# Batch 0's score maxima in two halves of heads on 64 partitions, and eight of its scores in the opening of each layer

## The chip, the cores and the metric

One core of a Trainium2 chip runs the kernel. The metric is the device time of one launch in microseconds, the median of three runs. A profile of one execution gives the rows quoted below; their times count from the start of its span. TensorE is written PE there, with its weight loads as PEld; VectorE is DVE, ScalarE is ACT, GpSimd is POOL, and SyncE (SP) only issues transfers.

## The reference, cut to what matters

Two layers of gated cross attention, each followed by a gated feed-forward part, on x of 4 batches x 512 queries x 128 channels, with a context of 154 keys, 16 heads of 8 channels. Layer 1 is causal.

```python
x = x + tanh(g_xattn[0]) * L0_xattn(layernorm(x), ctx, ctx)   # softmax(q k^T / sqrt(8)) v, 16 heads
x = x + tanh(g_ffn[0])   * L0_ffn(layernorm(x))               # quantised gate/up/down, needs maxima over all of x
x = x + tanh(g_xattn[1]) * L1_xattn(layernorm(x), ctx, ctx)   # the same with a causal mask
x = x + tanh(g_ffn[1])   * L1_ffn(layernorm(x))               # an LSTM-like scan over the batches
```

Every softmax is taken with its row maximum subtracted, so for each query and head the maximum over the keys is needed before the exponential.

## The kernel before

**Layout.** Heads are numbered h = 4g + j. Query tile Q4 and key tile Kd have 128 partitions = four strips of 32, one for each j; in a strip, 8 channels x 4 rows, which hold the query's high part twice, its low part, and (row 3 of each four) minus the maximum. Kd is a diagonal: for head (g, j) only strip j is filled and the other 96 partitions are zero, so a matmul over all 128 partitions gives one head's scores. There are three Q4 and three Kd tiles, used in rotation by the batches.

**Maxima.** For each batch, `scores_for_top` (L952) multiplies on TensorE one query tile of 128 queries with the keys of up to three heads (a unit: 462 columns of one PSUM bank; a unit that crosses a group g is two matmuls, for example 154 + 308). `UNITS` lists them: 22 for a batch of layer 0. In layer 1 there are 20, and those of the first 256 queries add a causal mask by a second matmul (L956). Three banks (`MRING`) rotate. `take_top` (L1323) reduces each bank on VectorE to `nm`. When the last is done, `split_top` (L1334, L1336) splits `nm` in a high and a low part `nms`; `turn_top` (L966) transposes them on TensorE; `copy_top` (L762) copies them on ScalarE to `nmT`; and SyncE's `tops` (L445) sends them into row 3 of each four in Q4, signalling `m_in`.

**Scores.** Then `scores` (L984, and L990 for the 26 keys left, "tail") makes 20 banks of 512 columns for the batch, on two rotating PSUM banks, `exps` (L771) takes each through the exponential on ScalarE into a ring of eight, and `weigh` (L1016) multiplies four at a time with the values, a "round", in shape 128x32, four column groups side by side.

**Order.** It is written out by hand. For each layer, a turn i runs from -1 to 4 with 20 slots each; turn i holds the scores of batch i and the maxima of batch i + 1, and the last three slots a first part of the maxima of batch i + 2 (8 units for batch 1). Turn -1 is the **opening**: only maxima of batch 0, with projections, values and, after each unit, a filler matmul (`fill`, L1082, 128 partitions, result unused). `PE_PLAN`, `ACT_PLAN` and `DVE_PLAN` place the rest by slot and batch. Engines execute in this order and wait on semaphores:

```python
if t == 0:
    pe.wait_ge(m_in[n % 3], 2 * 16 * (n // 3 + 1))          # scores: the batch's maxima have landed
...
if k >= MRING:
    pe.wait_ge(top_red, k - MRING + 1)                      # units: bank reduced three units before
```

**GpSimd** clears tiles, adds biases to the values (L580, L584), and for layer 1 zeroes masked exponentials (L619).

## Time and profile before

| | us |
|---|---|
| runs | 343.91, 344.22, 344.16; median 344.16 |
| profiled execution | 343.68, its span 341.7 |
| PE busy | 279.8 (82%) |
| DVE busy | 252.4 (74%) |
| ACT busy | 192.5 (56%) |
| POOL busy | 136.4 (40%) |
| DVE maxima, L1323, 168 reductions | 96.0, 626 ns each |
| ACT exponentials, L771, 148 | 82.3, 583 ns each |
| PE maxima, L952, 240 matmuls | 69.7 |
| PE scores, L984, 119 matmuls | 54.4 |

The difference between the profiled execution's time and its span, 2.0 us, lies outside the first and last instruction. Matmuls overlap, so the duration of one (some 0.4 us) is more than the distance from its start to the next one's start; where the text speaks of what a matmul takes, it is that distance. A load row stands at the moment at which the engine starts it, which is normally when the matmul ahead starts, so the load hides behind that matmul.

### The profile page before, as it was taken

To read this page: it belongs to the slowest core of one execution; us is meant where nothing else is said; L and a number is where in the kernel's file an instruction comes from. 1 tells how busy PE (TensorE), PEld (TensorE's weight loads), DVE (VectorE), ACT (ScalarE), POOL (GpSimd) and SP (SyncE) were. 2 spreads that over 40 slices of the span, in tenths; PEclk is the share of its full clock that TensorE was granted. 3 is DMA by queue.
4 is the path that set the end of the run, shared out by engine and by line. 5 is a ranking of instruction groups with operands and counts; after the bars stand their busy time and mean duration, and the time that the engine had idled before them with its cause. 6 is when DMAs were issued, how large, how long until landed. Compare 5 with 4: busy or idle time off the path is not lost. (4 is left out here: it accounts for less than half of the span.)

```text
span 341.7 us, 4467 instructions
## 1 busy us (share of the span) xinstructions
PE 279.8 (82%) x1424; PEld 161.2 (47%) x1424; DVE 252.4 (74%) x538; ACT 192.5 (56%) x303; POOL 136.4 (40%) x274
## 2 busy tenths in 40 slices
PE   0889899899989779985007888899998998999994
PEld 0558544545434355331006776574554653433552
DVE  5699876878997288799989968985696692442833
ACT  1673366566466656679589632356556546664232
POOL 6669893750040411860002059911486107140100
PEclk9999999999999999995556999999999999999998
DMA  7930100110000000000000002220011000000004
GB/s 209 326 150 3 69 32 10 41 60 9 1 10 1 0 2 0 1 0 0 1 0 0 2 14 78 94 101 1 10 59 48 2 0 11 0 1 2 0 1 123
DMA packets 9687, 12.55 MB, mean 37 GB/s; under 512 B 896, under 2 KB 5376, under 8 KB 9664
## 3 DMA queue, kind: packets, MB, share of 16 engines
q1 hardware_dynamic: 9232, 11.80, 9.7%
q10 hardware_dynamic: 432, 0.47, 0.7%
q8 instruction: 11, 0.18, 0.2%
q14 instruction: 12, 0.10, 0.1%
HBM read 4.27 MB, written 1.05 MB: 16 GB/s over the span
## 5 line engine op out<-in xcount | busy, mean ns | idle before, releaser
L1323 DVE TENSOR_REDUCE sb_nm<-ps_top 128x3 f32<-128x462 f32 (+2 forms) x168 | 96.0, 626 | 26.6 <-PE ps_top L952 13.7
L771 ACT ACTIVATE sb_pr<-ps_score 128x512 f32<-128x512 f32 (+1 forms) x148 | 82.3, 583 | 58.8 <-PE ps_score L984 49.2
L952 PE MATMUL ps_top<-sb_Kd,sb_Q 128*128 128x462 f32 (+3 forms) x240 | 69.7, 349 | 4.7 <-DVE sb_nm L1323 2.4
L984 PE MATMUL ps_score<-sb_Q,sb_Kd 128*128 128x512 f32 x119 | 54.4, 467 | 1.3 <-ACT sb_pr L771 1.0
L952 PEld LDWEIGHTS ps_top<-sb_Kd,sb_Q 128*128 128x128 f32 x240 | 42.6, 188 | 18.1 <-DVE sb_nm L1323 11.9
L625 POOL TENSOR_SCALAR sb_var<-sb_mv 128x4 f32<-128x4 f32 x16 | 4.6, 290 | 83.4 <-DVE sb_mv L1286 82.9
L984 PEld LDWEIGHTS ps_score<-sb_Q,sb_Kd 128*128 128x128 f32 x119 | 22.2, 188 | 31.7 <-ACT sb_pr L771 23.5
L1016 PE MATMUL ps_pv<-sb_pr,sb_V 128*32 128x512 f32 x256 | 34.1, 605 | 0.0
L619 POOL TENSOR_SCALAR_AFFINE_SELECT sb_pr<-sb_pr 128x512 f32<-128x512 f32 x16 | 10.5, 658 | 46.4 <-ACT sb_pr L771 46.4
L1343 DVE STREAM_TRANSPOSE sb_oq<-ps_pv 128x512 f32<-128x512 f32 x16 | 10.8, 700 | 12.4 <-PE ps_pv L1016 12.3
L642 POOL TENSOR_SCALAR sb_xn<-sb_xr,sb_nmean,sb_rstd 128x128 f32<-128x128 f32 x44 | 19.1, 448 | 1.1
L627 POOL TENSOR_TENSOR sb_rstd<-sb_var,sb_half 128x4 f32<-128x4 f32 x16 | 17.7, 1105 | 1.3
L520 POOL CAST sb_Kd<-sb_K 32x616 fp32r<-32x616 f32 x20 | 14.0, 702 | 8.5 <-DVE sb_K L1234 7.4
L1016 PE MATMUL ps_pv<-sb_pr,sb_VT 128*32 128x512 f32 (+1 forms) x128 | 14.9, 550 | 0.9 <-ACT sb_pr L771 0.9
L1094 PE MATMUL ps_top<-sb_wfT 128*128 128x256 f32 x30 | 9.8, 484 | 6.9 <-DVE sb_amax L1460 6.4
L990 PE MATMUL ps_score<-sb_Q,sb_KT 128*128 128x384 f32 (+1 forms) x29 | 13.0, 455 | 2.7 <-ACT sb_pr L771 2.7
L929 PE MATMUL ps_misc<-sb_consts,sb_xn 128*128 128x128 f32 x64 | 10.6, 290 | 5.3 <-POOL sb_xn L642 2.2
L1283 DVE BATCH_NORM_STATS2 sb_stat<-sb_xr 128x6 f32<-128x128 f32 x64 | 13.9, 280 | 1.4 <-DMA sb_xr<-x 1.2
L496 POOL MEMSET sb_Q<- 128x2048 f32 x1 | 1.8, 1804 | 32.6 <-DVE sb_amax L1460 32.6
L1185 PE MATMUL ps_top<-sb_front,sb_wfT 128*128 128x512 f32 x22 | 11.4, 650 | 2.7 <-ACT sb_uf L829 2.2
L603 POOL TENSOR_TENSOR sb_xg<-sb_xr,sb_bog 128x128 f32<-128x128 f32 x32 | 13.6, 457 | 0.1
L1076 PE MATMUL ps_misc<-sb_consts,sb_amx 128*128 128x128 f32 x8 | 2.5, 400 | 13.2 <-DVE sb_amx L1393 13.2
(180 smaller groups left out, 557.9 us busy)
## 6 DMA issues: line engine op xcount, KB each, us to landing
sb_Q<-sb_qh SPq DMA_DIRECT2D x16, 256.0 KB, 2.3
sb_Q<-sb_ql SPq DMA_DIRECT2D x8, 256.0 KB, 3.0
sb_xr<-x SPq DMA_DIRECT2D x4, 256.0 KB, 7.8
out<-sb_xr SPq DMA_DIRECT2D x4, 256.0 KB, 2.5
sb_wsb<-w SPq DMA_DIRECT2D x1, 704.0 KB, 9.3
sb_wf<-wffn SPq DMA_DIRECT2D x1, 576.0 KB, 9.2
sb_wkr<-wkr SPq DMA_DIRECT2D x2, 256.0 KB, 7.0
sb_Q<-sb_nmT SPq DMA_DIRECT2D x16, 32.0 KB
```

The lines of the kernel that those rows point to most:

```text
L520: ins = pool.tensor_copy(Kd[n % 3][q, :, j, :], K4[q, :, b, :])
L603: ins = pool.tensor_tensor(xg[:, n % 2, t, :], xr[:, TT * b + t, :], bog[:, layer, :], ALU.add)
L627: pool.tensor_tensor(rstd[:, k % 4, :], var[:, k % 4, :], half[:, :], ALU.pow).then_inc(rstd_r, 1)
L642: ins = pool.tensor_scalar(xn[:, kind == "post", t, :], xr[:, TT * b + t, :], nmean[:, k % 4, t:t + 1], rstd[:, k % 4, t:t + 1], ALU.add, ...
L771: act.activation(pr[:, k % PRING, q0:T], score_bank(B * layer + b, t)[:, q0:T], ACT.Exp, scale=SCALE).then_inc(exp_r, 1)
L952: ins = pe.matmul(cols[:, c0:c1, :], Q4[n % 3][:, g, P * qt:P * qt + P], Kd[n % 3][:, g, j:j + c1 - c0, 0:keys], start=True, stop=not mask ...
L984: ins = pe.matmul(ps[:, :], Kd[n % 3][:, g, j, 0:P], Q4[n % 3][:, g, :], start=True, stop=True, skip_group_check=True)
L990: ins = pe.matmul(ps[:, q0:T], KT[:, b, t - H, :], Q4[n % 3][:, t - H, q0:T], start=True, stop=(layer == 0), skip_group_check=True)
L1016: ins = pe.matmul(acc[32 * g:32 * g + 32, q0:T], lhs, pr[:, (TILES * n + t) % PRING, q0:T], start=(r in (0, 2)), stop=(r >= 4), skip_group ...
L1185: pe.matmul(fbank[t % FRING][:, :], wfT[:, 3 * (t // 12) + m, :], xq[:, c, :], start=True, stop=True).then_inc(fmm, 1)
L1283: ins = dve.bn_stats(stat6[:, k % 4, t, :], xr[:, TT * b + t, :])
L1323: dve.tensor_reduce(nm[:, :, :].rearrange("p t h -> p (t h)")[:, f0:f0 + heads], top[k % MRING][:, 0:keys * heads].rearrange("p (h k) -> p ...
```

## The change

1. Batch 0's maxima of each layer are cut in two halves of heads: first j = 0, 1 (partitions 0 to 63), then j = 2, 3 (partitions 64 to 127), 11 + 11 units in layer 0 and 10 + 10 in layer 1. Each such matmul uses only the 64 partitions of its half, and covers at most two heads, so that a unit of three heads is always two matmuls.
2. After the first half, `split_half`, `turn_half`, `copy_half` and `half_tops` bring its maxima into Q4 (slots 6 and 8 of turn -1), signalling `half_in`; the second half follows where the whole did before.
3. The first eight scores and exponentials of batch 0 (heads j = 0, 1) stand in slots 13 to 16 of turn -1, two a slot; the other twelve are spread over 20 slots of turn 0, and its rounds are at slots 0, 3, 9, 14 in place of 7, 10, 13, 17. The 16 scores of batch 0 that are not tails take 64 partitions too.
4. The five fillers at slot 13 go.
5. `values`: the bias is added for four batches in one instruction, 8 instructions in place of 32.

```diff
+HALF_SPLIT, HALF_TURN = 6, 8
+FIRST_SCORES = {13: (0, 1), 14: (2, 3), 15: (4, 5), 16: (6, 7)}
+LATER_SCORES = {0: (8,), 1: (9,), 3: (10,), 5: (11,), 7: (12,), 9: (13,), 10: (14,), 12: (15,), 15: (16,), 16: (17,),
+                18: (18,), 19: (19,)}
+FIRST_ROUND_AT = (0, 3, 9, 14)
...
+            def half_tops(layer, k):
+                n = B * layer
+                sp.wait_ge(nmT_r, top_no(layer, 0, k == 0) + 1)
+                for a in range(2):
+                    sp.dma_start(Q4[n % 3][64 * k + 3 + PARTS * a:64 * k + 64:32, :, :].bitcast(F32),
+                                 nmT[8 * a:8 * a + 8, k, :].bitcast(F32)).then_inc(half_in if k == 0 else m_in[n % 3], 16)
...
-                        for b in range(B):
-                            if t == 0:
-                                ins = pool.tensor_tensor(V4[:, b, :, j, 16 * (j % 2):16 * (j % 2) + D], src[:, b, :, j, :],
-                                                         bias[:, :, j, :], ALU.add)
...
+                        if t == 0:
+                            ins = pool.tensor_tensor(V4[:, :, :, j, 16 * (j % 2):16 * (j % 2) + D], src[:, :, :, j, :],
+                                                     bias[:, :, j, :].unsqueeze(1).to_broadcast([P, B, G, D]), ALU.add)
...
-                f0, heads, keys = UNITS[layer][u]
+                f0, heads, keys = (HALVED if b == 0 else UNITS)[layer][u]
+                own = slice(64 * (f0 // 32), 64 * (f0 // 32) + 64) if b == 0 else slice(0, P)
...
-                    ins = pe.matmul(cols[:, c0:c1, :], Q4[n % 3][:, g, P * qt:P * qt + P], Kd[n % 3][:, g, j:j + c1 - c0, 0:keys],
+                    ins = pe.matmul(cols[:, c0:c1, :], Q4[n % 3][own, g, P * qt:P * qt + P],
+                                    Kd[n % 3][own, g, j:j + c1 - c0, 0:keys],
...
+            def turn_half(layer, k):
+                pe.wait_ge(nms_r, top_no(layer, 0, k == 0) + 1)
+                fill_misc(pe, ("top" if k else "half", layer, 0))
...
-                if t == 0:
+                if (b, t) == (0, 0):
+                    pe.wait_ge(half_in, 32 * (layer + 1))
+                elif t == (H // 2 if b == 0 else 0):
                     pe.wait_ge(m_in[n % 3], 2 * 16 * (n // 3 + 1))
...
-                    ins = pe.matmul(ps[:, :], Kd[n % 3][:, g, j, 0:P], Q4[n % 3][:, g, :], start=True,
+                    own = slice(64 * (j // 2), 64 * (j // 2) + 64) if b == 0 else slice(0, P)
+                    ins = pe.matmul(ps[:, :], Kd[n % 3][own, g, j, 0:P], Q4[n % 3][own, g, :], start=True,
...
-                        if i == -1 and slot == LAST:
-                            fill(5)
...
+            def split_half(layer, k):
+                for t in range(TT):
+                    ins = dve.tensor_copy(part[0][:, t], src[:, t])
...
+                for t in range(TT):
+                    ins = dve.tensor_tensor(part[1][:, t], src[:, t], part[0][:, t].bitcast(F32), ALU.subtract)
```

**TensorE, layer 0's opening, around the projection of batch 2's queries.** Rows are one instruction or a run of like ones, with the size of the result. L952 are maxima, L1082 fillers, L935 a projection. Before:

```order
L952 MATMUL ps_top<-sb_Kd,sb_Q 128x308
L1082 MATMUL ps_score<-sb_maskr,sb_identr 128x256
L935 MATMUL ps_misc<-sb_xnT,sb_wsb 128x512
L952 MATMUL ps_top<-sb_Kd,sb_Q 128x308
L952 MATMUL ps_top<-sb_Kd,sb_Q 128x154
L1082 MATMUL ps_score<-sb_maskr,sb_identr 128x256
L952 MATMUL ps_top<-sb_Kd,sb_Q 128x462
L1082 MATMUL ps_score<-sb_maskr,sb_identr 128x256
```

After (L1017 are the maxima, on 64 partitions; L1159 fillers and L999 the projection, on 128):

```order
L1159 MATMUL ps_score<-sb_maskr,sb_identr 128x256
L999 MATMUL ps_misc<-sb_xnT,sb_wsb 128x512
L1017 MATMUL ps_top<-sb_Kd,sb_Q 128x154
L1017 MATMUL ps_top<-sb_Kd,sb_Q 128x308
L1159 MATMUL ps_score<-sb_maskr,sb_identr 128x256
L1017 MATMUL ps_top<-sb_Kd,sb_Q 128x308
L1017 MATMUL ps_top<-sb_Kd,sb_Q 128x154
L1159 MATMUL ps_score<-sb_maskr,sb_identr 128x256
```

Every unit is two matmuls now, and the 64-partition pairs alternate with 128-partition fillers: 43 changes of array shape ahead of the first score, 2 before.

**TensorE, the end of that opening.** After the last unit, before: six fillers, the turn (L966), early units of batch 1, of which the first four rows are shown.

```order
L952 MATMUL ps_top<-sb_Kd,sb_Q 128x154
L1082 MATMUL ps_score<-sb_maskr,sb_identr 128x256 x6
L966 MATMUL ps_misc<-sb_consts,sb_nms 32x128 x4
L952 MATMUL ps_top<-sb_Kd,sb_Q 128x462
L952 MATMUL ps_top<-sb_Kd,sb_Q 128x154
L952 MATMUL ps_top<-sb_Kd,sb_Q 128x308 x2
L952 MATMUL ps_top<-sb_Kd,sb_Q 128x154
```

After:

```order
L1017 MATMUL ps_top<-sb_Kd,sb_Q 128x308
L1159 MATMUL ps_score<-sb_maskr,sb_identr 128x256
L1061 MATMUL ps_score<-sb_Q,sb_Kd 128x512 x4
L1031 MATMUL ps_misc<-sb_consts,sb_nms 16x128 x4
L1061 MATMUL ps_score<-sb_Q,sb_Kd 128x512 x4
L1017 MATMUL ps_top<-sb_Kd,sb_Q 128x462
L1017 MATMUL ps_top<-sb_Kd,sb_Q 128x154
```

Eight scores (L1061) and the second half's turn now stand ahead of the early units of batch 1; on ScalarE the copy of the second half stands between the fourth and the fifth exponential.

**TensorE, layer 1's opening, units with a mask** (L956 before, L1022 after, on 128 partitions). Before:

```order
L952 MATMUL ps_top<-sb_Kd,sb_Q 128x462
L956 MATMUL ps_top<-sb_maskr,sb_identr 128x3x26
L1082 MATMUL ps_score<-sb_maskr,sb_identr 128x256
L952 MATMUL ps_top<-sb_Kd,sb_Q 128x154
L956 MATMUL ps_top<-sb_maskr,sb_identr 128x26
L952 MATMUL ps_top<-sb_Kd,sb_Q 128x308
L1082 MATMUL ps_score<-sb_maskr,sb_identr 128x256
```

After:

```order
L1017 MATMUL ps_top<-sb_Kd,sb_Q 128x256
L1022 MATMUL ps_top<-sb_maskr,sb_identr 128x256
L1017 MATMUL ps_top<-sb_Kd,sb_Q 128x256
L1022 MATMUL ps_top<-sb_maskr,sb_identr 128x256
L1159 MATMUL ps_score<-sb_maskr,sb_identr 128x256
L1017 MATMUL ps_top<-sb_Kd,sb_Q 128x256
L1022 MATMUL ps_top<-sb_maskr,sb_identr 128x256
```

Main and mask matmuls alternate, so each masked unit changes the shape four times: 61 changes ahead of layer 1's first score, 2 before. In batch 0's turn the count is 22 against 10 in layer 0 and 21 against 8 in layer 1; in the whole program 237 against 104.

## Rows read from the trace of the kernel before

**Rows 1.** Windows: stretch, length, busy of PE, PEld, DVE, ACT, POOL; PEclk, DMA, GB/s.

```profile
19.80:33.50 13.70, 12.41 (x77) 9.94 (x76) 12.52 (x28) 7.00 (x13) 12.62 (x35) 1.00 0.16 59
39.40:55.60 16.20, 15.71 (x84) 8.35 (x83) 10.60 (x21) 11.13 (x21) 12.13 (x27) 1.00 0.12 45
207.10:219.50 12.40, 12.16 (x65) 9.26 (x66) 11.18 (x24) 5.30 (x8) 11.72 (x15) 1.00 0.17 65
160.00:165.00 5.00, 0.31 (x1) 0.00 (x0) 5.00 (x10) 4.54 (x6) 0.00 (x0) 0.50 0.00 0
```

**Rows 2.** Timeline, TensorE, layer 0's opening: start, duration, engine, line, what.

```profile
21.06 0.52 PE L952 MATMUL ps_top<-sb_Kd,sb_Q 128*128 128x154 f32 x2 [0.73 <-ACT sb_maskr L796]
...
26.98 0.46 PE L952 MATMUL ps_top<-sb_Kd,sb_Q 128*128 128x308 f32 x2
27.43 0.38 PE L952 MATMUL ps_top<-sb_Kd,sb_Q 128*128 128x462 f32 x1
27.77 0.37 PE L952 MATMUL ps_top<-sb_Kd,sb_Q 128*128 128x462 f32 x1
```

**Rows 3.** Timeline, VectorE before and in layer 0's opening.

```profile
12.87 0.38 DVE L1286 BATCH_NORM_AGGREGATE sb_mv<-sb_stat 128x2 f32<-128x6 f32 x4
...
27.48 4.70 DVE L1323 TENSOR_REDUCE sb_nm<-ps_top 128x3 f32<-128x462 f32 x8 [0.20 <-PE ps_top L952]
```

**Rows 4.** Timeline, from the turned maxima to the first scores, layer 0.

```profile
35.19 0.61 PE L966 MATMUL ps_misc<-sb_consts,sb_nms 128*32 128x128 f32 x4 [0.85 <-DVE sb_nms L1336]
35.53 0.30 PEld L952 LDWEIGHTS ps_top<-sb_Kd,sb_Q 128*128 128x128 f32 x2
35.84 0.59 ACT L762 ACTIVATE sb_nmT<-ps_misc 32x512 fp32r<-32x512 f32 x1 [2.23 <-PE ps_misc L966]
36.05 8.83 DVE L1323 TENSOR_REDUCE sb_nm<-ps_top 128x3 f32<-128x462 f32 x16 [0.92 <-PE ps_top L952]
36.45 1.29 SPq L445 DMA_DIRECT2D sb_Q<-sb_nmT  x2
39.38 0.50 PE L984 MATMUL ps_score<-sb_Q,sb_Kd 128*128 128x512 f32 x1
39.91 4.65 ACT L771 ACTIVATE sb_pr<-ps_score 128x512 f32<-128x512 f32 x8 [3.49 <-PE ps_score L984]
```

**Rows 5.** Timeline, the last 2-partition matmuls (L1051) and what follows, layer 1.

```profile
322.86 0.38 PE L1051 MATMUL ps_pv<-sb_bfo,sb_onesr 2*128 2x512 f32 x1
323.09 0.39 PE L1051 MATMUL ps_pv<-sb_bfo,sb_onesr 2*128 2x512 f32 x1
323.41 0.52 PEld L1057 LDWEIGHTS ps_score<-sb_wsb,sb_pnT 128*128 128x128 f32 x4 [0.36 <-issue]
```

**Rows 6.** Timeline, around a round of 32-column matmuls, layer 0.

```profile
43.77 0.37 PE L952 MATMUL ps_top<-sb_Kd,sb_Q 128*128 128x462 f32 x1
44.06 1.06 PE L1016 MATMUL ps_pv<-sb_pr,sb_V 128*32 128x512 f32 x8
45.06 0.50 PE L984 MATMUL ps_score<-sb_Q,sb_Kd 128*128 128x512 f32 x1
45.40 0.37 PE L952 MATMUL ps_top<-sb_Kd,sb_Q 128*128 128x462 f32 x1
```

**Rows 7.** Timeline, layer 1: first unit, first early units of batch 1, scores.

```profile
207.19 0.48 PE L952 MATMUL ps_top<-sb_Kd,sb_Q 128*128 128x512 f32 x1 [0.90 <-issue]
222.13 0.48 PE L952 MATMUL ps_top<-sb_Kd,sb_Q 128*128 128x512 f32 x1
222.88 5.21 DVE L1323 TENSOR_REDUCE sb_nm<-ps_top 128x4 f32<-128x512 f32 x9 [1.18 <-PE ps_top L956]
226.32 0.70 PE L984 MATMUL ps_score<-sb_Q,sb_Kd 128*128 128x512 f32 x2
```

**Rows 8.** Timeline, GpSimd, half of the value biases of layer 0.

```profile
37.36 5.08 POOL L584 TENSOR_TENSOR sb_VT<-sb_tmp,sb_bvt 32x32 f32<-32x32 f32 x16
```

**Rows 9.** Timeline, a wait for an exponential in batch 0's turn, layer 1.

```profile
239.80 0.45 PE L990 MATMUL ps_score<-sb_Q,sb_KT 128*128 128x384 f32 x1 [0.73 <-ACT sb_pr L771]
```

118 lines of the change are left out of this document (90 added, 28 removed), and 1 row of the table PE_PLAN.

## The prediction

> **What bounds the kernel now.** I read the windows first [rows 1]. In both openings (19.8 to 33.5 and 207.1 to 219.5 us) VectorE is busy 12.5 of 13.7 and 11.2 of 12.4 us, and TensorE shows nearly as much. The timelines tell them apart. A unit of maxima with its filler takes TensorE 0.34 us when it is one matmul (27.43 to 27.77) and 0.45 us when it is two (26.98 to 27.43) [rows 2]; VectorE needs 0.59 us for a reduction there (8 in 4.70, hardly a wait between them) [rows 3] and 0.55 a little later (16 in 8.83) [rows 4]. So VectorE sets the pace of an opening, and TensorE has 0.1 to 0.2 us of slack a unit. At its end TensorE turns the maxima, ScalarE copies them (35.84), they travel (issue at 36.45), and the first score starts at 39.38, after eight early units of batch 1 at VectorE's pace [rows 4]. From 39.4 to 55.6 (batch 0's turn) TensorE is busy 15.7 of 16.2 us, ScalarE 11.1 and VectorE 10.6 [rows 1]: there TensorE is the bound. Layer 1 is alike, with its first unit at 207.19 and its first score at 226.32 [rows 7].
>
> **What the change removes.** Eight scores of batch 0 leave each turn in which TensorE is the bound. A 512-column matmul whose weights are loaded behind the one before takes 0.23 us (322.86 to 323.09) [rows 5], at times a little less; 8 x 0.22 = 1.8 us a layer. Eight exponentials leave with them; they were not the bound. The five closing fillers filled a wait. On GpSimd 24 of 32 bias additions go (the slower 16 take 5.08 us now, until 42.4 [rows 8]). The first round needs the values and now comes right behind score 8, which by the sum below is at 49.6, so it would find them ready with or without this edit. I cost both at nothing; without the later score 8 the edit would be worth having.
>
> **What it adds: changes of array shape.** Batch 0's matmuls, maxima and scores, now use 64 partitions of the array, while fillers, mask matmuls and other batches' units still use 128. No row of the trace has 64 partitions. Two changes of shape are near. (a) From 2 partitions back to 128: the last matmul of L1051 starts at 323.09 and streams until 323.31 or 323.32, but the next weight load starts only at 323.41. For 0.10 us the array runs empty, where within one shape the load would have started at 323.09 [rows 5]. (b) A round in 32 columns: the unit at 43.77 ends at 43.96, the round starts at 44.06, 0.10 again; and after it the score takes 0.34 (45.06 to 45.40), 0.11 over the 0.23 of rows 5, because nothing hides its weight load [rows 6]. So a change costs 0.10 + 0.11 = 0.21 us, and both directions are seen. One row speaks the other way: after the turned maxima (128x32), four at 0.11, the next load starts at 35.53, 0.34 after the first at 35.19, without a gap [rows 4]. Those are transposes; maxima and scores are ordinary matmuls like L1051, so I take 0.21, and keep 0 and 0.11 for the range.
>
> The Trainium skill (TensorEngine Tiling, Key Properties) says that a change of the tiling mode, not only of the tile, drains TensorE, and gives no price. The trace agrees in (a) and (b), does not in the transposes, and is silent on 64 partitions. If 64 partitions were exempt, the sum would be rival B's.
>
> **Opening of layer 0.** A unit is now two matmuls and stands alone between fillers. Streaming 462 + 256 columns is 0.30 us, two changes 0.42, the second matmul's load some 0.05: 0.77 us a unit, above VectorE's 0.59. TensorE becomes the bound. The second unit starts at 21.06, when the masks are there [rows 2]; 21 units take 16.2 us. TensorE's other work there: values in 2 x 8 matmuls of 0.11, 1.76; one turn 0.44; a projection, which like the round at 44.06 streams 512 columns four times, 0.88; and the new half turn 0.44 + 0.21 [rows 4, 6]; in all 3.73. The first score then starts at T = 21.06 + 16.2 + 3.7 = 41.0. VectorE's extra copies (eight small ones for each half; four small ones took 0.38 [rows 3], so 0.8, against a pair now) lie in its new idle time; were VectorE still the bound, they would cost about 0.8.
>
> **Eight scores paced by ScalarE.** With two banks a score waits for the exponential two before it. Exponential 0 is at T + 0.53, the pitch 0.58 (eight in 4.65), four end at T + 2.85; then ScalarE copies the second half's maxima, 0.59; two more exponentials end at T + 4.6 [rows 4]. Only there can the eighth score start; with it and a change of shape the first early unit starts at T + 5.1. VectorE, idle since about T + 1.4, starts 0.5 us later, five reductions end at T + 8.35, and behind the eighth unit score 8 starts at T + 8.65 = 49.6. Its rows (copied by T + 3.44, 2.9 us to landing as from 36.45 to 39.38) are there at T + 6.4. Before, score 0 stood at 39.38: 10.2 us late.
>
> **Batch 0's turn.** Less 1.8 for the scores, plus 12 x 0.21 = 2.5 for the changes (22 against 10, because each of the eight scores left on 64 partitions stands alone). Some waits for exponentials go; like the one of 0.73 in layer 1 [rows 9] they make up part of the turn, and I take 0.9 for them. Sum - 0.2. Layer 0: + 10.0.
>
> **Layer 1.** Ten of 20 units carry masks, which stay on 128 partitions, so each of these has four changes: four stream 1024 columns (0.43 + 0.84 = 1.27), six some 530 (0.22 + 0.84 = 1.06); ten plain ones take 0.77, six fillers on masked units 0.11 each: 5.1 + 6.4 + 7.7 + 0.7 = 19.9. One turn, two projections and the half turn add 2.85. First score at 207.19 + 22.75 = 229.9. The early units carry masks too (0.75 us from TensorE's start to VectorE's, 222.13 to 222.88, then 0.58 each, nine in 5.21 [rows 7]), so score 8 comes 9.35 later, at 239.3, against 226.32: + 13.0. The turn: - 1.8 + 13 x 0.21 - 1.4 for waits = - 0.5. Layer 1: + 12.5.
>
> **Sum.** 10.0 + 12.5 = 22.5 us. The profiled execution took 343.7 us (span 341.7), 0.5 under the median of 344.16, so 344.2 + 22.5 = **366.7 us**.
>
> **Rivals.** A, the forecast, with its errors: 0.02 us on some 130 changes is 3 us, the waits in both turns another 3: 359 to 374. 0.76.
> B, a change to 64 partitions costs nothing. VectorE stays the bound of the openings, its copies add 0.8, the first score comes at 34.2, score 8 at 42.9 (+ 3.5), and the turn gets 1.8 + 0.9 shorter: + 0.8 in layer 0, some + 1.0 in layer 1: 346. For it: no row has 64 partitions, and the transposes leave without a gap. Against it: L1051 and the rounds. 0.09.
> C, not slower: as B, and batch 0's turn, short of eight scores, loses all its waits as well. TensorE then needs some 12.8 us there, against 16.2 [rows 1], which gives back the 3.5 us of the late score 8. It decides at a turn of 12.7 us: below it the kernel is faster, above it slower; 344, give or take 1. Against it: four rounds and 18 units remain, and batch 1 needs its own maxima turned, copied and sent first. 0.05, of that 0.03 within 0.2%.
> D, the load is exposed but the array does not run empty (0.11 a change): a unit at 0.57 is level with VectorE; the first scores come near 36.5 and 224, in all + 11: 355. 0.07.
> E, the clock. It is granted at 1.00 (2.4 GHz) in both openings and in batch 0's turn, and was at its lower level (0.50) where TensorE was busy 0.3 of 5 us [rows 1]. With half of an opening spent on loads and an empty array it could be granted 1.2 GHz there; 10 us of streaming would double: 377 or more. 0.03.
>
> **Range.** 354 to 374 holds A and D; B, C, E and A's tails are left out, under 2 in 10. About 0.2% is what a measurement of this kernel can tell from no change. Faster by more: 0.02; within: 0.03; slower: 0.95.
>
> **What would show it.** Right: in the first opening a weight load starts about 0.10 us behind the end of every stream at which 64 and 128 partitions meet; a unit with filler takes about 0.77 us; VectorE waits for "PE ps_top" before nearly each reduction; the first score stands near 41, score 8 near 49.6, batch 1's first score near 65.5; in layer 1 a masked unit takes over 1 us. VectorE stands idle for some 4 us during the first eight scores whichever rival holds. Wrong: reductions still back to back (B, C or D); a PEclk below 9 in an opening (E); and if the openings come out as forecast but the turns shrink by over 2 us, my waits were mis-sized.

## The result, and the profile after

The changed kernel took 402.5 us in the median of its four executions (399.08, 399.63, 405.36 and 406.04), against 344.14 before. That is 1.160 times the time before, 95% interval 1.158 to 1.162; ratios here and below leave out executions over 1.5% above the fastest of the same kernel, here the two longer ones. The forecast was 366.7 us with a range of 354 to 374. The direction was right, and the median missed by 36 us. The profiled execution is the longest, 406.04 us (span 404.1). Its mean granted clock was 0.834; the others had 0.837, 0.848 and 0.855. So the clock fell in all four, but by these means the two shorter ones spent some 13 to 19 us less at the low level than the profiled one (an estimate: twice the missing share of the clock, times the span). Where and how long it was low is read from the profiled execution alone.

The page of the changed kernel, busy tenths and granted clock in 40 slices of 10.1 us:

```profile
core 0 of [0], span 404.1 us
PE   1999999988999887996105879999989999899995
DVE  4865345449789847888989963623568949352544
PEclk9975555559999999999656995555799999999999
```

Before, the only low stretch between start and end was at 155 to 186 us, where TensorE had little to do for the most part (busy 11.1 of 31 us; rows 1 show 160 to 165). Now there are two new low stretches, at 24.3 to 89.2 us and 242.7 to 287.1 us. Each starts in an opening and reaches into batch 0's turn, in layer 0 almost to its end. The same in windows (columns as in rows 1):

```profile
21.00:24.00 3.00, 2.51 (x11) 1.71 (x11) 2.51 (x7) 2.96 (x7) 3.00 (x3) 1.00 0.45 175
26.00:52.00 26.00, 26.00 (x72) 16.97 (x72) 11.24 (x25) 3.65 (x6) 14.07 (x41) 0.50 0.01 2
62.00:89.00 27.00, 25.63 (x73) 10.60 (x73) 10.91 (x20) 6.61 (x12) 0.00 (x0) 0.50 0.01 3
90.00:100.00 10.00, 8.59 (x46) 4.67 (x46) 9.09 (x24) 4.95 (x10) 5.90 (x11) 1.00 0.01 2
243.00:250.00 7.00, 7.00 (x17) 4.48 (x17) 3.06 (x5) 0.00 (x0) 6.64 (x10) 0.50 0.00 0
250.00:277.00 27.00, 27.00 (x65) 15.99 (x65) 11.46 (x24) 5.88 (x9) 6.44 (x10) 0.50 0.08 31
```

TensorE reads as busy 26.00 of 26.00 us at 0.50 (1.2 GHz). So a busy share near one is no sign here that the full clock is granted, and it hides the fall unless PEclk is read beside it.

The timeline of TensorE shows the first opening on both sides of the fall, and then the first scores (start, duration; `64*128` is the new array shape):

```profile
21.49 0.52 PE L1017 MATMUL ps_top<-sb_Kd,sb_Q 64*128 64x154 f32 x2 [0.53 <-ACT sb_maskr L855]
21.93 0.38 PE L1159 MATMUL ps_score<-sb_maskr,sb_identr 128*128 128x256 f32 x1
22.25 0.48 PE L1017 MATMUL ps_top<-sb_Kd,sb_Q 64*128 64x308 f32 x2
22.65 0.39 PE L1159 MATMUL ps_score<-sb_maskr,sb_identr 128*128 128x256 f32 x1
22.97 0.51 PE L1017 MATMUL ps_top<-sb_Kd,sb_Q 64*128 64x154 f32 x2
23.41 0.38 PE L1159 MATMUL ps_score<-sb_maskr,sb_identr 128*128 128x256 f32 x1
23.73 0.48 PE L1017 MATMUL ps_top<-sb_Kd,sb_Q 64*128 64x308 f32 x2
...
52.06 1.22 PE L1061 MATMUL ps_score<-sb_Q,sb_Kd 64*128 64x512 f32 x2
53.54 1.28 PE L1061 MATMUL ps_score<-sb_Q,sb_Kd 64*128 64x512 f32 x2 [0.26 <-ACT sb_pr L830]
...
58.39 4.42 PE L1017 MATMUL ps_top<-sb_Kd,sb_Q 128*128 128x462 f32 x12
62.74 0.79 PE L1061 MATMUL ps_score<-sb_Q,sb_Kd 64*128 64x512 f32 x1
```

While the clock was full, units followed each other at 0.76, 0.72 and 0.76 us (21.49, 22.25, 22.97, 23.73): the forecast's 0.77. Reckoned as in the prediction, the filler at 21.93 loads for 0.11 us and streams for 0.11 (its 256 columns pass through the array), until 22.15; the next unit starts at 22.25, so the 0.10 us of empty array fits too. After the fall a unit takes 1.2 to 1.3 us. VectorE waits for TensorE, as forecast. Its reductions from the opening's start to the first score, grouped by line (count; busy, mean; idle before them), in the kernel before (20 to 39 us) and in the changed one (20 to 52 us):

```profile
L1323 DVE TENSOR_REDUCE sb_nm<-ps_top 128x3 f32<-128x462 f32 (+1 forms) x28 | 15.6, 619 | 2.1 <-PE ps_top L952 1.9
```

```profile
L1403 DVE TENSOR_REDUCE sb_nm<-ps_top 128x3 f32<-128x462 f32 (+1 forms) x22 | 13.5, 622 | 15.4 <-PE ps_top L1017 15.3
```

Layer 1's opening, from its first unit at 241.47, had the full clock for 1.3 us only:

```profile
241.75 0.39 PE L1022 MATMUL ps_top<-sb_maskr,sb_identr 128*128 128x256 f32 x1
242.07 0.38 PE L1017 MATMUL ps_top<-sb_Kd,sb_Q 64*128 64x256 f32 x1
242.38 0.38 PE L1022 MATMUL ps_top<-sb_maskr,sb_identr 128*128 128x256 f32 x1
242.70 0.55 PE L1017 MATMUL ps_top<-sb_Kd,sb_Q 64*128 64x256 f32 x1
243.18 0.58 PE L1022 MATMUL ps_top<-sb_maskr,sb_identr 128*128 128x256 f32 x1
```

Until 242.70 a 256-column stream with its change takes 0.31 us, four of them 1.26, the forecast's 1.27 for a masked unit. From there it is 0.51.

Milestones of the profiled executions, in us from the start of the span ("warm" is the last experiment below):

| | before | forecast | changed | warm |
|---|---|---|---|---|
| first score, layer 0 | 39.38 | 41.0 | 52.06 | 45.80 |
| score 8 | 45.06 | 49.6 | 62.74 | 55.51 |
| batch 1's first score | 55.59 | 65.5 | 89.82 | 71.89 |
| first unit, layer 1 | 207.19 | 217.2 | 241.47 | 223.52 |
| batch 1's first score, layer 1 | 243.37 | 265.9 | 306.02 | 298.86 |
| end | 341.7 | 364.2 | 404.1 | 396.9 |

From batch 1's first score to layer 1's first unit it is 151.6 us before and after, and from batch 1's first score in layer 1 to the end 98.3 and 98.1. All of the 62.4 us therefore lies in an opening and the turn behind it: 34.2 in layer 0 and 28.4 in layer 1, less 0.3.

### The profile page after: what moved, and what is told of

It reads as the page before. It is cut to its first block and busy times, and to the rows that moved or that the text cites. A ratio compares the mean times of both kernels' runs of the same rounds, so it can differ in the third digit from the quotient of the medians.

```text
span 404.1 us, 4513 instructions
## 1 busy us (share of the span) xinstructions
PE 341.8 (85%) x1450; PEld 190.6 (47%) x1450; DVE 259.8 (64%) x566; ACT 194.5 (48%) x305; POOL 127.1 (31%) x226
## 5 line engine op out<-in xcount | busy, mean ns | idle before, releaser
L1403 DVE TENSOR_REDUCE sb_nm<-ps_top 128x3 f32<-128x462 f32 (+3 forms) x168 | 99.6, 628 | 80.6 <-PE ps_top L1017 53.3
L1017 PE MATMUL ps_top<-sb_Kd,sb_Q 128*128 128x462 f32 (+6 forms) x262 | 91.2, 423 | 3.3 <-DVE sb_nm L1403 1.6
L1017 PEld LDWEIGHTS ps_top<-sb_Kd,sb_Q 128*128 128x128 f32 (+1 forms) x262 | 55.4, 237 | 33.7 <-issue 18.8
L1061 PE MATMUL ps_score<-sb_Q,sb_Kd 128*128 128x512 f32 (+1 forms) x119 | 59.8, 524 | 2.1 <-ACT sb_pr L830 1.8
L1061 PEld LDWEIGHTS ps_score<-sb_Q,sb_Kd 128*128 128x128 f32 (+1 forms) x119 | 24.3, 209 | 37.5 <-ACT sb_pr L830 23.2
L1093 PE MATMUL ps_pv<-sb_pr,sb_V 128*32 128x512 f32 x256 | 37.6, 662 | 0.0
L1159 PE MATMUL ps_score<-sb_maskr,sb_identr 128*128 128x256 f32 x37 | 20.4, 552 | 0.0
L1440 DVE STREAM_TRANSPOSE sb_oq<-ps_pv 128x512 f32<-128x512 f32 x16 | 10.8, 700 | 12.4 <-PE ps_pv L1093 12.3
L1022 PE MATMUL ps_top<-sb_maskr,sb_identr 128*128 128x26 f32 (+4 forms) x54 | 18.6, 344 | 0.0
L799 ACT ACTIVATE sb_qh<-ps_misc,sb_cols 128x512 fp32r<-128x512 f32 x8 | 5.5, 688 | 24.6 <-PE ps_misc L999 24.6
L1363 DVE BATCH_NORM_STATS2 sb_stat<-sb_xr 128x6 f32<-128x128 f32 x64 | 13.9, 279 | 1.4 <-DMA sb_xr<-x 1.2
L1022 PEld LDWEIGHTS ps_top<-sb_maskr,sb_identr 128*128 128x128 f32 x54 | 12.4, 229 | 4.6 <-issue 2.9
```

The source lines that it names most:

```text
L1017: ins = pe.matmul(cols[:, c0:c1, :], Q4[n % 3][own, g, P * qt:P * qt + P], Kd[n % 3][own, g, j:j + c1 - c0, 0:keys], start=True, stop=not ...
L1022: ins = pe.matmul(cols[:, c0:c1, lo:keys], identr[:, :], maskM[:, 0:keys - lo].unsqueeze(1).to_broadcast([P, c1 - c0, keys - lo]), start=F ...
L1061: ins = pe.matmul(ps[:, :], Kd[n % 3][own, g, j, 0:P], Q4[n % 3][own, g, :], start=True, stop=True, skip_group_check=True)
L1093: ins = pe.matmul(acc[32 * g:32 * g + 32, q0:T], lhs, pr[:, (TILES * n + t) % PRING, q0:T], start=(r in (0, 2)), stop=(r >= 4), skip_group ...
L1159: pe.matmul(score[1][:, 0:256], identr[:, :], maskr[:, 0:256], start=True, stop=True, skip_group_check=True)
L1363: ins = dve.bn_stats(stat6[:, k % 4, t, :], xr[:, TT * b + t, :])
```

## The experiments

A matmul is called narrow here when it uses 64 (or fewer) of the 128 partitions, and wide when it uses all; a stream is a matmul seen as its columns passing through the array; the pitch is the time from one unit's start to the next one's. Unless it is said otherwise, times and ratios are against the kernel before, run beside each experiment (medians of 343.9 to 344.2 us). Two theories at first. **Gaps (G)**: each change of array shape leaves the array empty and a load exposed, less of an opening streams, and so the clock falls. **Narrow (N)**: it is the matmuls on 64 of the 128 partitions that count for less, with gaps or without.

**1. Changes without narrow work.**

```
+            def tiny():
+                pe.matmul(score[1][:, 0:16], identr[0:64, :], maskr[0:64, 0:16], start=True, stop=True,
+                          skip_group_check=True)
...
                                 fill(1)
+                                tiny()
```

> The kernel before, with one 16-column matmul on 64 partitions behind each filler of the two openings (its result is never read). Each adds two changes of array shape and next to no streaming; everything that counts stays on 128 partitions and in its old order. Two theories on why the granted clock of the changed kernel fell to 0.50 at 24.5 us. Theory G (gaps): what falls is the share of an opening in which columns stream; at two changes of 0.21 us a unit this kernel has the same pitch (0.34 to 0.45 + 0.42 = some 0.8 us) and the same share of streaming (0.3 of 0.8) as the changed one, so the clock falls to 0.50 in the first opening here too, stays low for tens of us, and the time is over 375 us. Theory N (narrow): it is the matmuls on 64 partitions themselves that count for less, and the share of streaming is high enough; here nearly all streaming is on 128 partitions, so PEclk stays at 9 and 1.00 in both openings. At a full clock the unit's pitch of 0.8 against VectorE's 0.59 adds some 0.2 us to each of 38 units: 344 + 8 = 352 us.

Measured: 1.031 times before (1.025 to 1.036), four executions at 353.1, 356.0, 361.9 and 363.7 us; the profiled one (353.1) was granted 1.00 in both openings:

```profile
24.00:34.00 10.00, 10.00 (x55) 7.66 (x54) 7.65 (x13) 1.34 (x3) 8.93 (x33) 1.00 0.08 29
```

Its units came every 0.73 to 0.77 us, the pitch of the changed kernel, and the clock held. That is against G as the sole cause. But the two longer executions (361.9 and 363.7 us) had mean clocks of 0.93 against 0.965. By that they spent some 25 us more at 0.50 than the profiled one (an estimate, worked out as above); no trace shows where. So gaps with next to no narrow streaming can lower the clock too, in some executions; what they don't do is to lower it each time and for as long as in the changed kernel (0.834 to 0.855).

**2. Narrow work without changes**, on the changed kernel.

```
-                    pe.matmul(score[1][:, 0:256], identr[:, :], maskr[:, 0:256], start=True, stop=True,
+                    ins = pe.matmul(bank[:, 0:256], identr[own, :], maskr[own, 0:256], start=True, stop=True,
...
-                                fill(1)
+                                h = 64 * (HALVED[layer][u][0] // 32)
+                                fill(1, slice(h, h + 64))
```

> The changed kernel, with each opening filler on the 64 partitions of the unit beside it (fillers of the second half write the other bank; the first score waits for the last filler). The first opening then has no change of shape between units and fillers, and the second only those at mask matmuls. Theory G: pitch of a unit back at VectorE's 0.59 us, the share of streaming as before the change (0.30 of 0.59), clock at 1.00 in layer 0; the second opening, where masked units keep two changes, may still fall; 350 to 365 us. Theory N: even less streaming on 128 partitions than in the changed kernel, so the clock falls at about the same place or earlier, and the time stays near 400 us.

Measured: 394.0 us (391.0 to 395.8), 1.145 times. Its control for the first opening is run 4, whose units and fillers have the same columns in the same order on all partitions. Timeline rows of both, first this run, then run 4:

```profile
21.08 0.37 PE L1018 MATMUL ps_top<-sb_Kd,sb_Q 64*128 64x308 f32 x2
21.45 0.41 PE L1018 MATMUL ps_top<-sb_Kd,sb_Q 64*128 64x154 f32 x2
21.85 0.48 PE L1018 MATMUL ps_top<-sb_Kd,sb_Q 64*128 64x308 f32 x2
22.40 0.52 PE L1018 MATMUL ps_top<-sb_Kd,sb_Q 64*128 64x154 f32 x2
23.60 0.75 PE L1018 MATMUL ps_top<-sb_Kd,sb_Q 64*128 64x308 f32 x2 [0.57 <-DVE sb_nm L1411]
```

```profile
21.57 0.37 PE L970 MATMUL ps_top<-sb_Kd,sb_Q 128*128 128x308 f32 x2
21.94 0.41 PE L970 MATMUL ps_top<-sb_Kd,sb_Q 128*128 128x154 f32 x2
22.35 0.48 PE L970 MATMUL ps_top<-sb_Kd,sb_Q 128*128 128x308 f32 x2
22.89 0.52 PE L970 MATMUL ps_top<-sb_Kd,sb_Q 128*128 128x154 f32 x2
24.10 0.41 PE L970 MATMUL ps_top<-sb_Kd,sb_Q 128*128 128x308 f32 x1 [0.56 <-DVE sb_nm L1341]
```

The steps are 0.37, 0.40, 0.55 and 1.20 us in the one and 0.37, 0.41, 0.54 and 1.21 in the other. The windows behind them, again in this order:

```profile
25.00:34.00 9.00, 9.00 (x39) 7.05 (x37) 5.79 (x17) 1.19 (x2) 8.13 (x31) 0.50 0.00 0
```

```profile
25.00:34.00 9.00, 9.00 (x67) 8.18 (x67) 8.13 (x16) 3.06 (x5) 8.01 (x32) 1.00 0.05 20
```

Up to 23.5 us both have the same columns and the same gaps; there the clock falls on 64 partitions, and on 128 it stays. That is one execution of each; the mean clocks of all four, 0.834 to 0.842 in this run and 0.935 to 0.953 in run 4, point the same way, though they cover both layers and, in this run, the narrow scores as well. For the first opening this speaks for N: narrow streams are enough there without any change of shape. In the second opening, where the changes at the mask matmuls stay, it fell too (235.1 us).

**3. and 4. The halved maxima alone, narrow and wide**, on the kernel before. Both runs take the changed kernel's `halved_units` and `halved_parts` for batch 0; in run 4 `own` is `slice(0, P)`.

```
+                own = slice(64 * (f0 // 32), 64 * (f0 // 32) + 64) if b == 0 else slice(0, P)
...
-                    ins = pe.matmul(cols[:, c0:c1, :], Q4[n % 3][:, g, P * qt:P * qt + P], Kd[n % 3][:, g, j:j + c1 - c0, 0:keys],
+                    ins = pe.matmul(cols[:, c0:c1, :], Q4[n % 3][own, g, P * qt:P * qt + P], Kd[n % 3][own, g, j:j + c1 - c0, 0:keys],
```

> The kernel before, with the maxima of batch 0 alone halved by heads, each half on 64 partitions; turn, rows, scores, rounds and biases stay as they were, fillers stay on 128 partitions (VectorE splits the maxima in eight small instructions instead of two). It shows whether the moved scores have a part in the fall of the clock. Under both theories the first opening has what the changed kernel has there, so the clock falls near 24 us. If the low stretch lasts because of the moved scores and the later turn, it is short here, and the time about 344 + 4 (pitch 0.77 against 0.59 for 21 units) + 5 in layer 1 + 10 for the low clock = 363 us; if it lasts whatever follows, over 380 us.

> The control of the run on maxima alone: the same halved units in the same order, with each matmul on all 128 partitions. No change of shape and nothing on 64 partitions: both theories say a clock of 1.00 in both openings. It has the halved units' second matmuls (a cut at every second head, in place of every fourth) and the eight small instructions at the split, 0.5 to 1 us a layer: 345 to 347 us. If the clock falls here as well, neither theory stands, and it is the number of matmuls and loads.

Measured: 384.5 us (1.118 times) on 64 partitions, 348.4 us (1.014, interval 1.011 to 1.016) on 128. Halving by heads costs 4.5 us; the 64 partitions, with the changes of shape that they bring beside wide fillers and masks, cost 36 more. The partitions that run 3 leaves out are ones in which Kd holds zeros for these heads; run 4 multiplies these zeros too, and has the shorter time. In run 4's second opening the clock was low as well, but for 3.4 us only (223.7 to 227.1), which was not expected. In run 3 the first score came at 57.06, and the turn behind it ran at 1.00 and took 16.2 us, as before the change [rows 1]:

```profile
30.00:57.00 27.00, 25.70 (x75) 17.50 (x74) 12.72 (x26) 3.64 (x6) 20.39 (x69) 0.50 0.02 7
57.00:73.00 16.00, 15.54 (x83) 8.37 (x82) 10.32 (x21) 10.87 (x21) 0.27 (x1) 1.00 0.12 47
```

The expectation that the clock would fall was right, its price (+ 10 us for a low stretch) far too small: the two stretches were 30.7 and 37.5 us long.

**5. The moved scores with wide maxima.**

```
-                own = slice(64 * (f0 // 32), 64 * (f0 // 32) + 64) if b == 0 else slice(0, P)
+                own = slice(0, P)
...
                 sp.wait_ge(nmT_r, top_no(layer, 0, k == 0) + 1)
+                sp.wait_ge(top_r, units_before(n) + 2 * HALF_UNITS[layer])
```

> The changed kernel with its order, turns, early scores and merged biases, but every maxima matmul of batch 0 on all 128 partitions; only its 16 scores stay on 64. So that the second half's maxima don't read rows that are being written, the first half's rows are sent only when the second half's last unit is done, which costs some 3 us ahead of the first score. It separates the order from the narrow maxima. If the narrow maxima made the clock fall (theory N after the first four runs), PEclk is 1.00 in both openings, units come every 0.59 us, and the eight scores paced by ScalarE end at about 34.5 + 3 + 8.6 = 46 us against 39.4 before: + 6 to 7 a layer, 357 us in all. If the order itself (TensorE waiting while ScalarE works off eight scores) lets the clock fall, the low stretch starts near 37 instead of 24 us, and the time is over 370.

Measured: 378.0 us (1.098 times). The opening was as expected (1.00). The clock fell at 37.6 us, in the wait before the first score, which this variant itself puts there, and stayed low through the turn, until 75.1:

```profile
35.40:38.60 3.20, 0.38 (x3) 0.15 (x3) 2.19 (x11) 0.16 (x1) 2.81 (x6) 0.84 0.03 13
40.00:50.00 10.00, 9.67 (x24) 5.47 (x24) 4.28 (x8) 4.35 (x9) 7.87 (x15) 0.50 0.21 82
```

So it says nothing on the order by itself; run 12 mends it.

**6. Only the scores narrow**, on the kernel before.

```
-                    ins = pe.matmul(ps[:, :], Kd[n % 3][:, g, j, 0:P], Q4[n % 3][:, g, :], start=True,
+                    own = slice(64 * (j // 2), 64 * (j // 2) + 64) if b == 0 else slice(0, P)
+                    ins = pe.matmul(ps[:, :], Kd[n % 3][own, g, j, 0:P], Q4[n % 3][own, g, :], start=True,
```

> The kernel before with nothing changed but batch 0's 16 scores, each on its 64 partitions; maxima and openings as they were. The turns of batch 0 get some 24 to 32 changes of shape instead of 10: at 0.21 us each, less what was waiting anyway, + 2 to 4 us a layer; at a full clock 350 us. Theory N: in the turn 16 x 0.21 = 3.4 of 16 us of streaming become narrow, while 18 units and the rounds stay as they are, so the clock may hold, and if it doesn't, it falls within batch 0's turn (40 to 56 us) and the time is over 360. A pure reckoning of gaps says the same places with less of a fall.

Measured: 372.6 us (1.084 times). The opening was at 1.00, and the fall came 3 us into the turn (42.6 us), with TensorE busy without a break; it lasted until 69.9:

```profile
39.40:45.00 5.60, 5.60 (x14) 2.66 (x15) 4.12 (x7) 3.12 (x6) 4.69 (x14) 0.79 0.18 69
50.00:55.00 5.00, 5.00 (x16) 2.34 (x16) 1.67 (x3) 1.79 (x3) 2.71 (x7) 0.50 0.00 0
```

Only these 16 scores, 3.4 of this turn's 16 us by the expectation, had become narrow; batch 1's maxima stayed wide. Narrow scores, with the changes of shape that they bring (35 in this turn's trace, 10 before), are enough to lose the clock. Which of the two does it, this run doesn't tell.

**7. More wide fillers in the changed kernel.**

```
-                                fill(1)
+                                fill(3)
```

> The changed kernel with three wide fillers behind each unit of the openings instead of one: two more streams of 256 columns on 128 partitions, 2 x 0.11 us, a pitch of 0.77 + 0.22 = 0.99 us at the full clock, nothing else. Theory N: what the clock wants is streaming on all partitions, which rises from 0.11 to 0.32 us a unit. If that is enough, the clock holds in both openings and the time is 367 + 41 x 0.22 = 376 us, faster than the changed kernel though it does more; if it isn't, the fall comes later or as before, and the low clock doubles the extra streams too: 400 us or more.

Measured: 405.1 us (1.178 times). The clock held through the whole first opening and fell at 47.1, in the eight scores:

```profile
21.00:45.00 24.00, 23.47 (x129) 17.09 (x127) 14.76 (x34) 7.10 (x14) 17.60 (x45) 1.00 0.09 35
55.00:65.00 10.00, 10.00 (x30) 3.56 (x29) 4.25 (x8) 1.79 (x3) 0.00 (x0) 0.50 0.01 2
```

The first score stood at 45.50; less 21 x 0.22 = 4.6 us of added fillers that is 40.9, against 41.0 in the forecast. Layer 0 kept what its opening gained: batch 1's first score stood at 82.47, 7.3 us earlier than in the changed kernel. Layer 1 lost it again. The clock was at 0.50 there from 238.3 us on for 47.8 us, the added fillers ran at that clock, and from the first unit to batch 1's first score it took 71.4 us against the changed kernel's 64.6.

**8. The merged value biases alone** (the same is done to the other half of the additions).

```
-                        for b in range(B):
...
-                                ins = pool.tensor_tensor(V4[:, b, :, j, 16 * (j % 2):16 * (j % 2) + D], src[:, b, :, j, :],
-                                                         bias[:, :, j, :], ALU.add)
+                            ins = pool.tensor_tensor(V4[:, :, :, j, 16 * (j % 2):16 * (j % 2) + D], src[:, :, :, j, :],
+                                                     bias[:, :, j, :].unsqueeze(1).to_broadcast([P, B, G, D]), ALU.add)
```

> The kernel before with the merged value biases alone (8 additions on GpSimd in place of 32, the same numbers added). I put this edit at nothing, because the first round found its values ready: 344.1, give or take 0.3. A rival: GpSimd free earlier lets its other work (keys, normalizing) start earlier, 342 to 343; or one wide addition with a broadcast operand is slower than four narrow ones, 345.

Measured: 344.3 us, 1.0005 times (0.9995 to 1.0014). It is worth nothing here, as forecast.

**9., 10., 13. and 14. The cost in dispute by itself.** 200 streams of 256 columns ahead of the first opening, on 64 (as below), 32 and all 128 partitions.

```
+                            for _ in range(200):
+                                pe.matmul(score[1][:, 0:256], identr[0:64, :], maskr[0:64, 0:256], start=True,
+                                          stop=True, skip_group_check=True)
```

> The disputed cost by itself. The kernel before, with 200 further streams of 256 columns behind each other on partitions 0 to 63, ahead of the first opening's units (results never read). No gap, no change of shape, nothing else on TensorE for 200 x 0.107 = 21.3 us. Theory G (only gaps count): TensorE has never been fuller, the clock stays at 1.00, 344 + 21 = 365 us. Theory N: a stream on 64 partitions counts for less. If it counts for half, a full stream of it may be just enough or just short of it; a fall shows as PEclk 5 within the 21 us or right behind them, and then the time is over 385 us.

> The same 200 streams on partitions 0 to 31 only. Theory G: 1.00 throughout, 365 us. Theory N, in proportion to the partitions: a quarter counts, so that the clock falls to 0.50 within the streams even if it held on 64; the rest of the streams then take 0.21 us each, and the time is over 385 us. If it holds on 32 as well, the number of partitions by itself is not it.

> The control of the streams: the same 200 streams of 256 columns ahead of the first opening, on all 128 partitions. If the share of partitions is what counts, the clock stays at 1.00 in every execution and the time is 344 + 21 = 365 us with a spread of 1 us. If it falls here too, in some executions, it is VectorE's and ScalarE's idleness or the place that lets it fall, and the streams on 64 and 32 partitions prove nothing.

> The same streams on partitions 0 to 63, in six executions more. Of two so far one took 387 and one 368 us. If half the partitions count for about half and this is just enough or just short of it, the executions fall into two groups again, near 368 and near 387 us. If 387 us was a disturbance, all are near 367.

| partitions | executions (us) |
|---|---|
| 128 | 367.3, 369.6, 370.2, 370.7 |
| 64 | 367.9, 367.9, 368.0, 368.1, 370.8 and 385.2, 386.8, 387.0 |
| 32 | 385.9, 387.8 |

A profiled execution on 64 that held, one on 64 that fell, and one on 32:

```profile
22.00:43.30 21.30, 21.30 (x180) 21.30 (x179) 0.00 (x0) 2.00 (x3) 10.87 (x34) 1.00 0.06 24
```

```profile
24.00:64.00 40.00, 40.00 (x188) 39.78 (x188) 0.49 (x1) 0.29 (x1) 9.12 (x33) 0.50 0.00 1
```

```profile
26.00:62.00 36.00, 36.00 (x169) 35.77 (x168) 0.35 (x1) 0.00 (x0) 7.15 (x29) 0.50 0.00 1
```

TensorE is as full as it can be in all of them. By their mean clocks (0.95 to 0.97 where it held, 0.90 to 0.91 where it fell), the clock held in four of four on all partitions, in five of eight on 64, and in none of two on 32. So no gap and no change of shape is needed for a fall, and the order of the counts is that of N. They are few: four of four against five of eight could well be chance, and on 32 there are only two. That the number of partitions counts rests on these counts together with runs 2 and 4. Both profiled falls came early, 2.3 and 4.2 us after the streams' start (21.46 and 21.12 us), behind a wait of 0.7 us for the mask, which the wide streams of run 13 had too. The 40 us at 0.50 show one more thing: the same streams that keep the full clock in one execution don't win it back in another. (A stream took 0.12 us, not 0.107, which is why the undisturbed ones stand at 368 and not at 365.)

**15. Both halves by turns.**

```
+                            for k in range(200):
+                                half = slice(64 * (k % 2), 64 * (k % 2) + 64)
+                                ins = pe.matmul(score[k % 2][:, 0:256], identr[half, :], maskr[half, 0:256],
+                                                start=True, stop=True, skip_group_check=True)
```

> The same 200 streams, by turns on partitions 0 to 63 and 64 to 127, each half writing its own bank, so that one needn't wait for the other. Either the two halves stream at the same time, then the 200 take 10.7 us in place of 21.3, the whole array is in use, the clock holds, and the time is 344 + 11 = 355 us; or one half waits for the other, then it is as the streams on 64 partitions: 21.3 us, 365 us if the clock holds and 387 if not.

Measured: 356.2 us (356.0 to 358.4), 1.037 times. The 200 streams took 12.2 us (21.17 to 33.35), two at once, the second of each pair starting 3 ns behind the first. Most of them:

```profile
22.00:33.50 11.50, 11.50 (x193) 11.37 (x190) 0.00 (x0) 1.98 (x3) 10.43 (x33) 1.00 0.12 44
```

The clock held in all four executions. So two narrow streams on opposite halves cost no more than one. That they also count as a wide one is not shown: on one half alone five of eight held, and these stretches are half as long. The Trainium skill (TensorE: Matmul & The Clock Gate, Part 3: Packing small matmuls) says that matmuls on different row groups run concurrently; this run agrees. The changed kernel hardly gets it: the neighbours of a narrow matmul are wide, or on the same half.

**11. The kernel before without fillers.**

```
-                            if i == -1 and FILL_FROM[layer] <= slot < LAST:
-                                fill(1)
```

> The kernel before without the filler behind each unit of the openings (the five closing ones stay). All matmuls are on 128 partitions, and VectorE sets the pace as before, 0.59 us a unit, so nothing is saved or lost in either opening by itself: 344 us if the clock holds. It shows how near the openings of the kernel before are to a fall: streaming goes from 0.30 to 0.19 us of each 0.59. Theory N in its stronger form (narrow streams count for nothing or half): the changed kernel had 0.11 wide and 0.19 narrow of 0.77, and this one has more on all partitions than that; it may hold. If the clock falls here as in the changed kernel, 380 us, the fillers are what keeps it up, and a narrow unit beside one wide filler is a unit too few.

Measured: 345.7 us, 1.004 times (1.001 to 1.006). The clock falls at 24.0 us here too, but is back after 6.8 us; it falls for 3.4 us twice more, at 41.0 in batch 0's turn and at 225.4 in layer 1's opening. So the fillers do help to hold the clock, and it can fall with everything wide. But with everything wide each fall was short, and VectorE, the bound, hardly notices it. In the changed kernel TensorE had become the bound, and VectorE waited for it for 15.3 us before the first score (2.1 us in the kernel before; the lines stand with the result).

**12. and 16. The order at the full clock**: run 5 with wide late scores and wide fillers in the waits; then the changed kernel with its narrow maxima and the same help (`fill(4)` in place of `fill(24)`, and `fill(3)` behind each unit).

```
                 if (b, t) == (0, 0):
+                    fill(24)
...
-                    own = slice(64 * (j // 2), 64 * (j // 2) + 64) if b == 0 else slice(0, P)
+                    own = slice(0, 64) if b == 0 and t < H // 2 else slice(0, P)
+                    if b == 0 and t < H // 2:
+                        pe.matmul(ps[:, 0:256], identr[:, :], maskr[:, 0:256], start=True, stop=True,
+                                  skip_group_check=True)
```

> The order of the changed kernel at the full clock. As the run with the changed order and wide maxima, but 24 wide fillers cover the wait before the first score, each of the eight early scores has a wide filler ahead of it in its own bank (within ScalarE's pace of 0.58 us a score), and the later eight scores of batch 0 are on 128 partitions. If the narrow matmuls and the idle stretch are all that lowers the clock, PEclk is 9 or 1.00 through both openings and turns. Then the first score stands near 38 us and score 8 at 38 + 8.6 = 46.7, against 39.4 for the first before: + 7 us a layer, less 2.7 for the shorter turn: 344 + 9 to 14 = 353 to 358 us. If it falls in the turn all the same, the order has a share of its own: over 365 us.

> The changed kernel with its narrow maxima, its order and its eight narrow early scores, and with wide streams added: three fillers behind each unit of the openings, four before the first score, one ahead of each of the eight early scores; the later eight scores of batch 0 are on 128 partitions. The openings with three fillers held the clock in layer 0 (first score at 45.5 us, of which 21 x 0.22 = 4.6 us are the added fillers: 40.9). If the clock now holds through most of the turns, the time is the forecast for the changed kernel, 366.7, plus about 41 x 0.22 = 9 us of added fillers, less 2 us for the changes that the later scores no longer make, plus some 5 us for short falls: 374 to 380 us. If it is near 400, the order or the narrow scores keep the clock down whatever fills the waits.

Measured: 365.5 us (1.062 times) and 398.4 us (1.157 times). In run 12 the clock was full but for 6.8 and 3.4 us in layer 0's turn and two stretches of 3.4 us in layer 1. The first score stood at 39.13, score 8 at 49.07 (+ 9.9 us, not 8.65), batch 1's first at 66.83, 11.2 us later than before. So the order costs at most 21 us in both layers; that figure holds the halving (4.5 us, run 4), the added fillers, the changes of shape at the eight early scores, the short falls, and this variant's own wait (3 us a layer by the expectation of run 5, not measured). I had expected 353 to 358. The eight scores were slower (0.74 us each with their filler, not 0.58), and the turn was not shorter: from score 8 to batch 1's first score it took 17.8 us, where 13.5 (16.2 less 2.7) had been expected; most of the 10 low microseconds lie in it.

Run 16 is the nearest test of the forecast in layer 0, because the clock held there nearly throughout. The third row below is layer 1:

```profile
21.00:45.00 24.00, 23.65 (x128) 17.38 (x129) 14.68 (x31) 6.80 (x12) 17.52 (x46) 1.00 0.09 35
45.00:68.00 23.00, 20.85 (x103) 10.84 (x101) 14.36 (x33) 10.51 (x18) 7.87 (x15) 0.99 0.10 37
235.00:245.00 10.00, 10.00 (x29) 6.64 (x27) 4.41 (x14) 3.43 (x5) 2.77 (x4) 0.50 0.21 79
```

Its first score, less 4.6 + 0.4 us of added fillers, is at 40.8. Batch 1's first score is at 71.89; less those 5.0 and 1.1 for the slower eight scores it is 65.8, against the forecast's 65.5. That it agrees to 0.3 us is partly luck. Behind score 8 this run has 8 changes of shape where the changed kernel has 21, 2.7 us by the forecast's price, and it had 3.4 us at the low clock, worth 1.7 us at most; neither was measured by itself. Put in, they give 66.8 to 68.5. In layer 1 the clock was at 0.50 from the first units for 58 us, in spite of the fillers; masked units have four changes and only some of them a filler. From the first unit to batch 1's first score it took 75.3 us there, against 36.2 before, and that is most of this run's 54 us. Which of narrow streams and gaps decides in layer 1 was not separated.

## Why the prediction was wrong

**Steps that held.** "Changes of array shape" at 0.21 us: the pitch of 0.72 to 0.76 us at the full clock in the changed kernel, 0.31 us a masked stream, and run 1. That ordinary matmuls behave like L1051 and the rounds, and not like the transposes, was the right choice; rivals B, C and D are out. (C's 12.8 us for the turn also has no working: 15.7 busy less 1.8 for the scores is 13.9.) "Opening of layer 0": 41.0 forecast, 40.8 and 40.9 where the clock held, less the added fillers. Merged biases at nothing: run 8. VectorE idle during the eight scores: 4.9 us, until 59.18. The sum for layer 1 (+ 12.5) was never seen at the full clock.

**Terms that were too small.** "Eight scores paced by ScalarE": from the first to score 8 it was 9.7 (run 16) and 9.9 us (run 12) instead of 8.65, though with a filler ahead of each, so the changed kernel's own figure at the full clock is not known; in it, at the low clock, 10.7. "Batch 0's turn": from score 8 to batch 1's first score the forecast has 15.9 us, and run 16 took 16.4 with 13 changes fewer and 3.4 us at the low clock, which makes 17.4 to 19.1 (an estimate). So the sum for layer 0 was 1 to 3 us short, and the miss of 36 us has another cause.

**The step that failed** is the clock. Every term of the sum is priced at 1.00, and a fall was left to rival E, at a chance of 0.03. E had the sign right and the place, the openings, but put the fall down to "loads and an empty array". Run 2 took those gaps out of the first opening, and the clock fell all the same; with gaps but nearly no narrow streaming (run 1) it held in the profiled execution. E went wrong in two numbers as well. Its chance came from reading rows 1 to mean that the clock falls where TensorE has next to nothing to do. No row of before has a matmul on 64 partitions, so the rows could not say that the full clock survives them, and this unknown had to carry a chance of its own, as B's and D's did. And its price, "10 us of streaming would double", took the low clock to end with the opening. In the profiled execution it lasted 64.9 us in layer 0 and 44.4 in layer 1. Two things that the runs show fit this: batch 0's turn is narrow as well (with a wide turn, run 3, the stretch in layer 0 was 30.7 us; with narrow scores alone, run 6, 27.3), and streams that could have kept the full clock don't bring it back (run 9). 109 us at half the clock can cost up to 54 us where TensorE is the bound (an estimate); that execution's span is 40 us beyond the 364.2 of the forecast. Why the chip grants less for narrow matmuls stays open.

**What the share of each cause is.** Alone and against before: halving by heads 4.5 us (run 4), narrow maxima with their changes of shape 36 on top (run 3), narrow scores with theirs 28 (run 6), the order at nearly full clock at most 21, which holds the halving and this variant's own wait and fillers (run 12), the biases 0 (run 8). That is more than the 58 us of the whole change, since one fall of the clock serves several of them; a share for each can't be given.

## What to carry to other kernels

Matmuls on a part of the partitions saved TensorE nothing by themselves (a 256-column stream took 0.12 us on 64 partitions and on 128), cost 0.21 us at each change of shape, and put the clock of everything around them at risk; leave them wide, or try them in pairs on opposite halves (run 15). Before an edit thins out what TensorE does (fewer partitions, more waits), look at PEclk and ask which wide streams hold the clock; if none of the trace's rows has the new kind of work, give the fall a real chance and price it over the whole stretch until the next dense wide work. And a stage whose bound is another engine forgives a fall (run 11: 1.5 us), while one where TensorE has just become the bound pays in full (a unit 1.2 to 1.3 us in place of 0.72 to 0.76).

## What was not expected of the hardware

- In these runs the granted clock depends on how many partitions the matmuls use, and not only on how full TensorE is: openings alike in columns and gaps went to 0.50 on 64 partitions and stayed at 1.00 on 128 (runs 2 and 4), and 200 streams back to back held 1.00 in 4 of 4 executions on 128 partitions, in 5 of 8 on 64 and in 0 of 2 on 32.
- What was granted before matters too: 40 us of gapless streams on 64 partitions stayed at 0.50, although in five of eight executions the same streams kept the 1.00 with which they began. The Trainium skill (TensorE: Matmul & The Clock Gate, What's actually happening) has the gate set by how busy TensorE has been recently; if busy is what the profile counts as busy, the runs on 64 and 32 partitions, 40.00 of 40.00 and 36.00 of 36.00 us at 0.50, show that this is not the whole of it, and the measurement decides.
- Two streams on opposite halves of the partitions start together and take 0.12 us as a pair, as long as one.
- The profile shows TensorE as busy 26.00 of 26.00 us at 0.50, with 72 matmuls in them, 2.8 a us; the opening before the change, busy 12.4 of 13.7 us at 1.00, had 77, 5.6 a us [rows 1].
